# x turned by DRAM from chunk 3 on, its norm spread over rows through DRAM, and the order of chunks 2 to 6 laid out anew

## What is computed

```python
x = x + attn(layernorm(x))     # gates, recurrence over 2048 steps, RMS norm
x = x + ffn(layernorm(x))      # 256 -> 1024 -> 256, dequantised weights, silu

pre = einsum('btd,df->btf', x, W) + b          # x: (2, 2048, 256), W: (256, 1024)
i_pre, f_pre, o_pre, z = split(pre, 4)
i = 10 * tanh((i_pre + input_bias) / 10); f = -softplus(f_pre)
m_next = max(f + m, i)                          # per step
c = exp(f + m - m_next) * c + exp(i - m_next) * tanh(z)
n = exp(f + m - m_next) * n + exp(i - m_next)
h = sigmoid(o_pre) * c / (n + 1e-6)
out = h / sqrt(mean(h * h) + 1e-8) * scale
```

## Time and profile before

| what | value |
|---|---|
| median of 3 runs | 321.74 us (321.66 to 321.97) |
| profiled execution | 321.89 us, its span 320.0 us |
| mean granted clock of PE | 0.989 of full speed |
| PE busy | 303.9 us (95%) |
| DVE busy | 267.4 us (84%) |
| ACT busy | 229.7 us (72%) |
| POOL busy | 118.1 us (37%) |

### The profile page before, as it was taken

How to read it: one execution, slowest core, us unless ns; L and a number is a source line. 1 busy time by engine, 2 the same in 40 slices (tenths; PEclk the granted TensorE clock), 3 DMA queues, 4 the chain that set the end, 5 groups by cost and what they waited for, 6 DMA issues and landing times.

```text
span 320.0 us, 4813 instructions
## 1 busy us (share of the span) xinstructions
PE 303.9 (95%) x1760; PEld 263.8 (82%) x1760; DVE 267.4 (84%) x474; ACT 229.7 (72%) x372; POOL 118.1 (37%) x126
## 2 busy tenths in 40 slices
PE   0999999999899997999999999999999999999996
PEld 0787788887898877988899888988899899899896
DVE  3998999999999999998969987888959899863531
ACT  3598966999599938489694978779593876941930
POOL 2162035002483179015920187014991156154000
PEclk9999998999999999799999999999999999999999
DMA  7990000000000020020000200010000100100101
GB/s 274 357 374 14 1 0 2 0 0 0 2 1 2 33 98 3 34 98 2 1 2 33 98 0 2 33 36 0 1 2 25 43 0 0 68 0 5 63 0 68
DMA packets 10951, 14.21 MB, mean 44 GB/s; under 512 B 688, under 2 KB 10160, under 8 KB 10672
## 3 DMA queue, kind: packets, MB, share of 16 engines
q1 hardware_dynamic: 10512, 13.12, 11.8%
q10 hardware_dynamic: 416, 0.79, 0.7%
HBM read 9.71 MB, written 4.19 MB: 43 GB/s over the span
## 4 chain that ended last, share of the span: by engine, by line
PE 45%; DVE 20%; issue 14%; POOL 12%; ACT 6%; DMA 3%; POOLq 0%; DVEq 0%; SPq 0%
PE mm_ps L221 7%; PE mm_ps L219 7%; PE mm_ps L220 7%; PE z_ps L220 6%; PE z_ps L219 6%; PE z_ps L221 6%; POOL rows L1034 3%; DVE rec L672 2%; DVE g L729 2%; DMA rows<-x 2%; POOL rec L1001 2%; DVE rows L737 2%; POOL g L1019 2%; DVE bn L742 2%; DVE rec L687 2%
## 5 line engine op out<-in xcount | busy, mean ns | idle before, releaser
L219 PE MATMUL z_ps<-w_hi,y_hi 128*128 128x256 f32 x248 | 71.3, 288 | 1.4 <-issue 1.4
L220 PE MATMUL z_ps<-w_lo,y_hi 128*128 128x256 f32 x248 | 70.4, 284 | 0.0
L221 PE MATMUL z_ps<-w_hi,y_lo 128*128 128x256 f32 x248 | 70.4, 284 | 0.0
L765 DVE TENSOR_TENSOR y_lo<-y,y_hi 128x512 fp32r<-128x512 f32 x64 | 43.2, 687 | 12.2 <-ACT y_hi L504 11.7
L501 ACT ACTIVATE y<-mm_ps,b_all 128x512 f32<-128x512 f32 x60 | 41.3, 688 | 13.4 <-PE mm_ps L288 9.8
L219 PEld LDWEIGHTS z_ps<-w_hi,y_hi 128*128 128x128 f32 x248 | 47.5, 191 | 1.9 <-issue 1.8
L220 PEld LDWEIGHTS z_ps<-w_lo,y_hi 128*128 128x128 f32 x248 | 47.2, 190 | 0.1
L221 PEld LDWEIGHTS z_ps<-w_hi,y_lo 128*128 128x128 f32 x248 | 47.1, 190 | 0.0
L1005 POOL TENSOR_TENSOR rrms<-meansq,minus_half 128x4 f32<-128x4 f32 x8 | 9.0, 1122 | 96.5 <-DVE meansq L723 96.5
L219 PE MATMUL mm_ps<-gt_hi,w_hi 128*128 128x512 f32 x108 | 43.2, 400 | 0.0
L220 PE MATMUL mm_ps<-gt_lo,w_hi 128*128 128x512 f32 x108 | 42.8, 396 | 0.0
(11 more groups left out here) (154 smaller groups left out, 669.4 us busy)
## 6 DMA issues: line engine op xcount, KB each, us to landing
out<-rows SPq DMA_DIRECT2D x15, 256.0 KB, 2.1
rows<-x SPq DMA_DIRECT2D x7, 512.0 KB, 6.4
q<-fc_q SPq DMA_DIRECT2D x2, 1024.0 KB, 12.1
s<-fc_scales SPq DMA_DIRECT2D x1, 1024.0 KB, 11.2
wg_raw<-fc_scales SPq DMA_DIRECT2D x1, 1024.0 KB, 11.1
wg_raw<-w_gates SPq DMA_DIRECT2D x1, 512.0 KB, 5.5
wg_raw<-w_gates ACTq DMA_DIRECT2D x1, 512.0 KB, 5.8
rows<-x ACTq DMA_DIRECT2D x1, 256.0 KB, 3.4
```

Of the source, the lines that this page charges most:

```text
L219: pe.matmul(dst, wh[w_at], ah[a_at], start=start, stop=False)
L220: pe.matmul(dst, wh[w_at], al[a_at], start=False, stop=False)
L221: return pe.matmul(dst, wl[w_at], ah[a_at], start=False, stop=stop)
L765: dve.tensor_tensor(y_lo[:, j], y[:, j % YBUFS], y_hi[:, j].bitcast(F32), ALU.subtract).then_inc(y_lo_done, 1)
```

## The change

From chunk 3 (`SPREAD`) on x no longer passes PE. A second input holds x already transposed, and SP loads a chunk of it into `xc`, [128, 2, 512]. The norm is then one factor and one shift for each column, the same in all 128 rows: SP stores these 1024 numbers to DRAM, and loads them back into all rows (`spread`). POOL multiplies `xc` by the factors and adds the shifts, in two instructions of 1024 elements. ACT and DVE split `xc` from SBUF as they split `t_ps` before. `xc` and `spread` lie in the place of `s1`, the scales of fc1, and there is one of each.

```diff
+xc = s1[:, 0].rearrange("p (k m) -> p k m", m=T)
+spread = s1[:, 1].rearrange("p (w m) -> p w m", m=T)
...
+            def load_turned(c):
...
+                    sp.wait_ge(xt_lo_done, at(c - 1, 2, 2))
+                sp.dma_start(xc, xt_view[c % SEQS, c // SEQS]).then_inc(xc_landed, 16)
+
+            def spread_norm(c):
+                sp.wait_ge(ln1_r, at(c, 2, 2))
+                sp.dma_start(norm_rows[c].rearrange("w t p -> p w t"), rn1[:, c % 2],
+                             allow_slow_non_contiguous=True).then_inc(norm_stored, 16)
+                sp.wait_ge(norm_stored, at(c - SPREAD, 16, 16))
...
+                    sp.wait_ge(xc_done, c - SPREAD)
+                sp.dma_start(spread, norm_rows[c].rearrange("w t p -> w (t p)").partition_broadcast(P)
+                             ).then_inc(norm_landed, 16)
...
             for c in range(CHUNKS):
+                if 1 <= c and exists(c + 4):
+                    spread_norm(c + 4)
...
                     load_x(c + XBUFS)
+                    load_turned(c + XBUFS)
...
+            def x_normalised(c):
+                def across(w):
+                    return spread[:, w].unsqueeze(1).to_broadcast([P, KD, T])
+
+                pool.wait_ge(xc_landed, at(c - SPREAD, 16, 16))
+                pool.wait_ge(norm_landed, at(c - SPREAD, 16, 16))
+                pool.tensor_tensor(xc, xc, across(0), ALU.mult).then_inc(xc_scaled, 1)
+                pool.wait_ge(xc_scaled, c - SPREAD + 1)
+                pool.tensor_tensor(xc, xc, across(1), ALU.add).then_inc(xc_done, 1)
```

The order of the loop on PE, DVE and POOL (only lines that change stand with a sign):

```diff
             for t in range(4, CHUNKS - 1):
                 gates(t, range(GJ))
+                fc2(t - 3, range(0, 2))
                 g_turned(t - 2)
-                fc2(t - 3, range(0, 2))
-                x_turned(t + 1)
                 fc2(t - 3, range(2, TT))
+                fc1(t - 2, range(0, 2))
                 h_turned(t - 1)
-                fc1(t - 2, range(KF))
+                fc1(t - 2, range(2, KF))
...
             for t in range(4, CHUNKS - 1):
                 ln1_root(t + 1)
                 base(t - 3)
+                x_normalised(t + 1)
                 rms_root(t - 1)
```

More of the change, by code:

```diff
@@ L32 @@
 YBUFS = 4
+SPREAD = 3
 def at(c, per, k):
@@ L384, in _ @@
             fc1(0, range(0, 6))
-            x_turned(3)
+            h_turned(1)
             fc1(0, range(6, KF))
-            gates(3, range(0, 2))
-            h_turned(1)
-            gates(3, range(2, GJ))
+            gates(3, range(GJ))
             fc2(0, range(0, 3))
@@ L549, in _ @@
             silu(0, range(2, 4))
+            square_sums(1)
             silu_alone(0, range(4, KF))
             act.preload_act_table_set("sigmoid_and_others")
[L553 to L558, removed]
+            gates(3, range(GJ))
             act.preload_act_table_set("natural_log_exp_and_others")
@@ L561, in _ @@
             g_normalised(1)
-            x_normalised(4)
             g_high(1)
@@ L573, in _ @@
             for t in range(4, CHUNKS - 1):
[L574 to L577, removed]
+                gates(t, range(GJ))
                 act.preload_act_table_set("natural_log_exp_and_others")
@@ L580, in _ @@
                 exp_i(t)
+                g_high(t - 2)
                 x_high(t + 1)
                 act.preload_act_table_set("silu_and_others")
+                silu(t - 2, range(0, 2))
                 square_sums(t - 1)
-                silu(t - 2, range(KF))
+                silu(t - 2, range(2, KF))
                 act.preload_act_table_set("sigmoid_and_others")
@@ L682, in divisor, with numerators @@
                                          op0=ALU.mult, op1=ALU.add).then_inc(denom_ready, 1)
-            def numerators(c):
+            def numerators(c, blocks=range(KD)):
                 s = c % 2
-                for k in range(KD):
+                for k in blocks:
                     dve.tensor_tensor_scan(rec[s][:, 2, k], f_gate[:, s, k], rec[s][:, 2, k], carry[:, s, 2, k:k + 1],
                                            ALU.mult, ALU.add).then_inc(num_done, 1)
+                if blocks[-1] < KD - 1:
+                    return
                 dve.wait_ge(num_done, at(c, 2, 2))
@@ L827, in _ @@
             h(0)
-            dve.wait_ge(w1_rounded, KD)
-            dve.tensor_tensor(w1_lo[:], w1_f, w1_hi[:].bitcast(F32), ALU.subtract).then_inc(w1_ready, 1)
+            ln1(3)
             maximum(1, range(0, 1))
             mean_square(0)
-            ln1_sums(3)
+            maximum(1, range(1, KD))
             dve.wait_ge(row_in, 16)
@@ L838, in _ @@
             ln2(0)
-            ln1_means(3)
-            maximum(1, range(1, KD))
             denominators(1, range(KD))
+            divisor(1)
             dve.wait_ge(beta_w1, 1)
@@ L844, in _ @@
                               ).then_inc(b1_ready, 1)
-            divisor(1)
+            numerators(1, range(0, 1))
             g_low(0)
-            numerators(1)
+            numerators(1, range(1, KD))
+            newton(1)
             o_times_c(1)
-            newton(1)
             refined(1)
@@ L854, in _ @@
             x_low(3)
+            y_low(0, range(2, 4))
+            mean_square(1)
             dve.wait_ge(q2_in, 16)
```

105 lines of the change are left out of this document (66 added, 39 removed).

## The result

The changed kernel took 361.33 us (360.45 to 362.25, 4 runs) against 321.74 us before: 1.123 times as long, with an interval of 1.120 to 1.126. The forecast was 327.6 us, in a range of 317 to 334. Its sign was right, its size was not: the loss is 39.6 us and not 5.9.

The account below looks back on a forecast made before the run. PE seemed the bound, but DVE had no room before 128 us and would be held by POOL. To the 320.0 us span it added 4.9 before chunk 5's gates and 0.8 in two passes, plus 1.9 outside: 327.6, range 317 to 334.

Parts of the forecast that it names:

- What bounds the kernel: PE seems the bound, but in chunks 1 to 4 DVE is as full: busy 87.1 of 89.8 us until 128.1.
- What PE wins: Five times eight transposes go, 0.79 us each chunk, 3.95 us; with nothing else binding, 9.1 us in all.
- The 2.05 and 1.7 us: PE's idleness ahead of chunk 5's transposes and the half clock after it, both to go if nothing else binds.
- The second rival: w1_lo on POOL costs nothing either, as DVE keeps its place: another 6.3 us, 312.7; chance 0.05.
- w1_lo on POOL: Chunk 2's gates: POOL blocks DVE, the divisor starts near 33.1, PE waits 4.6 us longer, plus 1.7 half clock.
- The pair: POOL's two xc instructions hold DVE 2.2 us for chunk 3, 4.2 for chunk 4; chunk 5's, behind `base`, take nothing.
- w2_hi: Its rounding on POOL, 3.3 us at most, costs DVE 1.3 beside the scaling of h.
- The order on DVE: Five instructions stand ahead of g(2)'s low part, 5.2 us, and the bias waits 1.3 us for POOL's `base`.
- DMA: Factor and shift out to DRAM and in again take 4.2 to 12.8 us; 7 taken, hidden behind `base`.
- the third rival: The DRAM round trip takes 10 us or more, delaying chunks 5, 6, 7 by 2.5 us each: 335; chance 0.17.
- The sum: Chunk 5's gates start at 152.9, set by DVE, +4.9 us; two passes +0.4 each; the rest stays; 327.6.
- the sum's line by PE: PE's limit for chunk 5's gates: 147.96 less transposes and waits, plus w1_lo's 4.6 and 1.7, gives 146.7.

Follow-up runs that it names:

- the path with the pair shrunk: Kernel before with only the new path of x (32-byte store, old order), POOL's multiplication and addition on xc shrunk to 4 elements each: 319.38 us (0.992).
- the nearest run: Changed kernel with w1_lo back on DVE, the store in 32-byte pieces, and POOL's two instructions on xc shrunk to 4 elements each: 325.34 us (1.010).
- the new path alone: Kernel before with only x's new path (turned x from DRAM, 32-byte store, POOL's two instructions on xc); order, w1_lo and w2_hi as before: 342.46 us (1.063).
- the base: Changed kernel with w1_lo back on DVE and the store in 32-byte pieces: 349.63 us (1.086).
- The one-input rows: Kernel before with only x's new path, POOL's two instructions on xc each reading one tensor and a scalar per row: 328.25 us (1.019).
- the pair shrunk in this kernel: Changed kernel, 4-byte store and w1_lo on POOL kept, POOL's two instructions on xc shrunk to 4 elements each: 342.04 us (1.062).
- the second move: Kernel before, chunk 5's transposes after three fc2 tiles, and in that pass bias and first half of `final` behind x's low part: 319.86 us (0.9945).

## Why the prediction was wrong, step by step

*What bounds the kernel.* Right: DVE before 128 us. With the path at nearly no price PE's saving was kept back there, and came through only in the passes.

*What PE wins.* The 0.79 us per chunk is about right (0.9 per pass). The 2.05 and 1.7 us were not to be had by taking the transposes out of the way: POOL's g and DVE's h were late as well, as the path with the pair shrunk showed, and as moving the transposes did. The second rival's 312.7 us (POOL at no price) was too low for the same reason; the nearest run gave 325.3 with the new order.

*w1_lo on POOL.* Right in place, and by itself in size (6.3 us in all for 6.3, with a wait of 3.98 us; 4.57 in the changed kernel). Wrong as a term of this sum: the new order had 3.48 us of another wait close behind, and some 2.0 us are what the edit is worth in it.

*The pair.* The first large miss, in three parts. Its length was taken from one row of 2.41 us, though the row beside it in the earlier trace rows had 2.78; in the changed kernel its two instructions took 2.6 to 3.5 us. Its hold was put at 2.2 and 4.2 us for chunks 3 and 4, and chunk 5's pair was said to take nothing before the low part of g(2). With the new path alone the rows show 5.7, 5.3 and 5.4 us in chunks 3, 4 and 5 (5.1, 4.2 and 5.3 in the base), in part on a copy of two or four elements, for which the sum had no charge. In the changed kernel itself the late store moved chunk 5's pair behind g(2): it held two scans, which took 6.65 us instead of 2.45. And its lateness had no term at all: POOL's pair stood in front of x's high part on ACT and of the next roots in POOL's own queue, 5.6 to 6.7 us per chunk. The sum had 7.7 us with w2_hi, where the runs show 23.1 without it; w2_hi itself took POOL 1.90 us (3.3 at most foretold), and the scaling of h beside it was not held. That a copy with one input can be held is what the Trainium skill says ("SBUF — State Buffer", section "Who interferes with whom": `copy` can, on conditions, take both port pairs); I had weighed only the half of the rule on two inputs. The same section lets the second to issue wait for the whole instruction. The row of the COPY agrees: it ended with POOL's instruction. The one-input rows differ: DVE's L753, issued at 61.80 beside POOL's 3.30 us from 61.19 on, was longer by 0.8 and ended at 63.82, before POOL did.

*The order on DVE.* 6.5 us foretold, 6.1 measured for the order of the passes, but not where the sum had it, so that the agreement is luck. With the pair shrunk PE's wait for the low part of g(2) and 5.3 us before chunk 5's gates are there, as the sum had them. With the pair the order costs nothing before chunk 5's gates, most likely since the pair had made h as late as g (PE waits 7.93 us for h in the old order, 8.68 for g in the new); it costs 3.6 and 2.1 us in the passes, where the sum had 0.4 each. Moving the low part of g back alone returned 2.3. Which other row of that order holds the rest was not taken apart.

*DMA.* The second large miss. The nearest rows were of large pieces, and their bounds of 4.2 to 12.8 us did not hold for 4-byte ones: 8.7 to 11.2 for the store and 4.1 for the load, 13.7 in the pass shown, where the sum had 7, hidden. "10 us or more" was the third rival's point, with chance 0.17. Its price of 7.5 us (2.5 for each of three chunks) is near the measured 7.6 (9.7 with w1_lo on DVE), of which 2.6 and 3.0 us lie in the passes and the rest behind them. What neither the forecast nor the rival had is the loop: silu stands behind x's high part and the next norm behind silu, so the delay is paid in every pass, until something else takes over. The rival's 335 us still fell 26 short, because it stood on the forecast's sum with its 7.7 us for the pair.

*The sum.* Forecast 152.9 for chunk 5's gates, measured 170.75, and the store has no part in that (170.81 with the fast one). The low part of g(2) ended at 153.98, where the sum had 142.0, and from there to the gates it was 16.8 us for 10.9, with 2.9 us of waits for ACT's silu and a granted clock of 0.84 from 150 to 171 us. With the pair shrunk in this kernel the gates start at 158.64: the pair has 12.1 us where the sum had 7.7. The rest of the miss was not taken apart whole. One part is a saving that did not come: the path with the pair shrunk starts them at 147.46, where the sum's line by PE, without w1_lo, gives 140.4. Passes of 37.0 foretold, 43.5 and 43.7 measured. The rest "stays" was wrong by 3.6 us.

## What to carry to other kernels

Before you hide a round trip, follow who waits for its end and who starts it again: if that closes, add up the loop and hold it against the pass. A long two-input instruction on POOL has two prices, what DVE loses beside it and what stands behind it in POOL's queue; here each was larger than the transposes that it saved. And when a wait goes, ask what is late next: here a wait of 2.05 us moved on to the next product, and it took the second move to win 1.8 us.

## What the runs showed of the hardware

A store of 1024 pieces of 4 bytes held the queue for 8.7 to 11.2 us; the same 4 KB in 128 pieces of 32 bytes took 1.4 in four of five (3.0 in the fifth, issue to issue). The changed kernel's 6048 packets under 512 B are mostly these.

A DVE copy of two elements took 2.91 us beside POOL's 1024 of two inputs, and 0.90 beside 1024 of one input; alone it took 0.17. POOL's 1024 elements issued 1.2 us before the end of a DVE scan took 4.13 us, against 2.6 to 3.5 in the changed kernel. With POOL's work cut into 256 elements, DVE's instructions took 1.90 instead of 1.22 us, and POOL's a mean of 1.62 and 1.26 us: neither engine was shut out, both lost time.

With a stepped read on POOL (eight elements apart) the multiplication took a mean of 3.02 us in the base against 3.00 in the kernel after, the addition 3.92 against 3.08. DVE's work beside the two differs as well, so that the step is not shown as the cause.
